# A gated attention and feed-forward kernel: the feed-forward stage written out, and two weight chunks split ahead of it

## The reference, cut to what matters

```
# x: [16, 512, 512], ctx: [16, 77, 512], float32 throughout
x = x + tanh(g_xattn) * attention(layernorm(x), ctx)       # 16 heads of 32
x = x + tanh(g_ffn) * ffn(layernorm(x))

def ffn(x):                                     # 512 -> 2048 -> 512
    hidden = x @ W1 + b1
    q = hidden + (cos(theta)*w_real + sin(theta)*w_imag) * w_imag * sin(theta + 0.1*hidden) * 0.1
    return relu(q) @ W2 + b2
```

## Time and profile before

| | |
|---|---|
| median of 3 runs | 2230.28 us (2228.26 to 2232.8) |
| the profiled execution | 2231.27 us, of which the span is 2229.5 us |
| PE, PEld busy | 98%, 82% of the span |
| DVE, ACT, POOL busy | 65%, 54%, 18% of the span |
| mean granted TensorE clock | 0.997 |
| feed-forward stage | from 812.7 us to the end |

### The profile page before, as it was taken

How to read it: one execution, slowest core, us unless ns; L and a number is a source line. 1 busy time by engine, 2 the same in 40 slices (tenths; PEclk the granted TensorE clock), 3 DMA queues, 4 the chain that set the end, 5 groups by cost and what they waited for, 6 DMA issues and landing times.

```text
span 2229.5 us, 30530 instructions
## 1 busy us (share of the span) xinstructions
PE 2183.2 (98%) x10385; PEld 1825.2 (82%) x10385; DVE 1438.1 (65%) x2596; ACT 1211.1 (54%) x3571; POOL 397.8 (18%) x329
## 2 busy tenths in 40 slices
PE   8989999999999989999999999999999999999999
PEld 6778888888888867888888788788888878888887
DVE  4566776676677648656656666566566566665654
ACT  3477777777777746444454444444444444544444
POOL 4033343333333311101101001011011010010110
PEclk9999999999999999999999999999999999999999
DMA  7513233333323334312223123122131231231210
GB/s 223 184 38 98 81 87 87 99 83 83 99 80 88 92 127 113 76 53 61 64 51 76 58 57 76 58 38 75 44 72 57 57 77 57 57 76 54 41 38 19
DMA packets 267311, 170.29 MB, mean 76 GB/s; under 512 B 189124, under 2 KB 203817, under 8 KB 267167
## 3 DMA queue, kind: packets, MB, share of 16 engines
q1 hardware_dynamic: 265775, 167.62, 28.2%
q0 software_dynamic: 960, 0.64, 0.2%
q10 hardware_dynamic: 432, 0.04, 0.0%
HBM read 108.86 MB, written 59.38 MB: 75 GB/s over the span
## 4 chain that ended last, share of the span: by engine, by line
PE 60%; DVE 1%; ACT 1%; DMA 1%; issue 0%; SPq 0%; ACTq 0%
PE m_bank L56 30%; PE pair_bank L56 30%; DVE w_split L1355 0%; DMA w_chunk<-in_L_ffn_W_dram 0%; DMA quad_scratch<-x_in 0%; DVE hidden L1388 0%; ACT relu L1315 0%; DVE turns L1384 0%; SPq L1199 0%; ACT hidden L1324 0%; ACT turns L1326 0%; DVE sine L1381 0%; DVE stats L173 0%; ACT w_split L1311 0%; DVE relu L1371 0%
## 5 line engine op out<-in xcount | busy, mean ns | idle before, releaser
L56 PE MATMUL m_bank<-xT,w_split 128*128 128x512 f32 x3072 | 740.7, 390 | 13.3 <-issue 9.4
L56 PE MATMUL pair_bank<-w_split,relu 128*128 128x512 f32 x3072 | 738.5, 389 | 3.6 <-DVE relu L1371 3.5
L56 PEld LDWEIGHTS m_bank<-xT,w_split 128*128 128x128 f32 x3072 | 577.5, 188 | 135.7 <-issue 11.5
L56 PEld LDWEIGHTS pair_bank<-w_split,relu 128*128 128x128 f32 x3072 | 576.2, 188 | 125.5 <-issue 3.8
L1331 ACT ACTIVATE sine<-turns 128x512 f32<-128x512 f32 x256 | 161.8, 632 | 386.2 <-DVE turns L1384 386.2
L1007 ACT ACTIVATE exps<-pair_bank,exp_bias 128x77 f32<-128x77 f32 x1024 | 319.5, 368 | 61.6 <-DVE exp_bias L1053 61.5
L1315 ACT ACTIVATE relu<-hidden 128x512 fp32r<-128x512 f32 x256 | 161.9, 632 | 348.3 <-PE m_bank L56 265.0
L1371 DVE SCALAR_TENSOR_TENSOR relu<-hidden,relu 128x512 fp32r<-128x512 f32 x256 | 181.2, 708 | 212.6 <-ACT relu L1315 212.6
L1388 DVE SCALAR_TENSOR_TENSOR hidden<-sine,sine_gain,hidden 128x512 f32<-128x512 f32 x256 | 197.2, 770 | 169.9 <-ACT sine L1331 169.9
L1007 ACT ACTIVATION_READ_ACCUMULATOR exps<-pair_bank,exp_bias 128x1 f32 x1024 | 255.4, 249 | 0.0
L193 POOL TENSOR_TENSOR rstd<-var_eps,minus_half 128x4 f32<-128x4 f32 x32 | 38.3, 1196 | 1202.2 <-DVE var_eps L189 1202.2
(11 more groups left out here) (117 smaller groups left out, 1918.8 us busy)
## 6 DMA issues: line engine op xcount, KB each, us to landing
x_in<-in_x_dram SPq DMA_DIRECT2D x16, 1024.0 KB, 5.7
residual<-in_x_dram SPq DMA_DIRECT2D x64, 256.0 KB, 2.7
x_scratch<-residual SPq DMA_DIRECT2D x64, 256.0 KB, 2.1
x_in<-x_scratch SPq DMA_DIRECT2D x16, 1024.0 KB, 5.6
residual<-x_scratch SPq DMA_DIRECT2D x64, 256.0 KB, 3.8
out_dram<-residual SPq DMA_DIRECT2D x64, 256.0 KB, 2.1
quad_scratch<-x_in SPq DMA_DIRECT2D x60, 256.0 KB, 5.6
x_in<-quad_scratch SPq DMA_DIRECT2D x60, 256.0 KB, 4.7
```

What stands on the lines that cost most here:

```text
L56: mm = pe.matmul(out, stationary(s), moving(m), start=first and n == 0, stop=last and n == len(PASSES) - 1)
```

## The change

1. In the feed-forward stage `over_batches` and SyncE's loop become Python loops: all 16 batches are written out for every engine.
2. Chunks 0 and 1 of w1 are split in attention. ScalarE writes their hi parts into `xT[1][0]` after its last turn; VectorE writes their lo parts into `xT[1][1]` behind the gating of output tiles 0 and 1. In the feed-forward stage ScalarE and VectorE start with chunk 2. The counts of the semaphores `chunk_hi` and `chunk_split` are raised by 3 with it.
3. TensorE takes slices 0 to 3 of batch 0 from `xT[1]`.
4. GpSimd begins the feed-forward stage with two copies, one per part, of all of `xT[1][i]` (128x2048) into `w1_split[i]`. `x_hi` of batch 1 and the first product of batch 1 wait for them (`early_kept`).

```
+        def early_parts(n):
+            return (w_chunk[n][:, :].rearrange("p (k f) -> p k f", k=KT),
+                    *(xT[1][i][:, :, HT * P * n:HT * P * (n + 1)] for i in range(2)))
...
                 over_batches(act, turn)                       # attention, ScalarE
+                for n in range(EARLY):                        # EARLY = 2
+                    raw, hi, _ = early_parts(n)
+                    act.wait_ge(chunk_loaded[n], 16)
+                    act.activation(hi, raw, ACT.Copy).then_inc(early_hi, 1)
...
                 for tile, n, bank in outputs_after():         # attention, VectorE
                     gate_output(B - 1, tile, n, bank)
+                    if tile < EARLY:
+                        raw, hi, lo = early_parts(tile)
+                        dve.wait_ge(early_hi, tile + 1)
+                        dve.tensor_tensor(lo, raw, hi.bitcast(F32), ALU.subtract).then_inc(early_split, 1)
...
-                batch(0, 0, False)                            # feed-forward, all engines
-                with eng.Fori(1, B - 2, 2) as b:
-                    batch(b, 1, False)
-                    batch(b + 1, 0, False)
-                batch(B - 1, 1, True)
+                for b in range(B):
+                    batch(b, b % 2, b == B - 1)
...
-                with sp.Fori(1, B - 2) as b:                  # SyncE
+                for b in range(1, B - 2):
...
+                pool.wait_ge(early_split, EARLY)              # GpSimd, first in its program
+                for i in range(2):
+                    pool.tensor_copy(w1_split[i][:, :, 0:EARLY * HT * P], xT[1][i][:, :, :].bitcast(F32)).then_inc(early_kept, 1)
...
-                        if f % HT == 0:                       # TensorE, first_product
+                        if f < EARLY * HT:
+                            pe.wait_ge(early_split, f // HT + 1)
+                        elif f % HT == 0:
                             pe.wait_ge(chunk_split, w1_number[f // HT] + 1)
                     elif f == 0:
                         pe.wait_ge(t_split, KT * b)
+                        if b == 1:
+                            pe.wait_ge(early_kept, 2)
...
+                        early = b == 0 and f < EARLY * HT
+                        mm = matmul3(pe, m_bank[f % 2][:, :], lambda p: (xT[1] if early else w1_split)[p][:, kt, f * P:(f + 1) * P],
...
+                    if b == 1:                                # ScalarE, x_hi
+                        act.wait_ge(early_kept, 2)
...
-                for n in range(STAGED):                       # ScalarE and VectorE, before step(0, 0)
-                    weight_lo(n)
+                for n in range(EARLY, STAGED):
+                    weight_lo(n)
+                dve.wait_ge(y_ready, NT)
```

## The result

| | before | after |
|---|---|---|
| median | 2229.27 us (4 runs) | 2215.9 us (2214.94 to 2216.13, 4 runs) |
| ratio | | 0.9942, 95% interval 0.9927 to 0.9957 |
| the profiled execution | 2231.27 us | 2215.73 us |

The kernel is 13.4 us (0.6%) faster by the medians; 2218 with a range of 2214 to 2224 was forecast. The median before has one run more here than ahead of the prediction, so it is 2229.27 and not 2230.28. In a second series, on another chip, the changed kernel had a median of 2215.09 and a ratio of 0.9931 (0.9918 to 0.9945).

What follows compares the result with a forecast made beforehand. TensorE, busy 98% of the span, was taken as the bound. 2231.27 - 11.1 (jumps) - 1.6 (start) = 2218.6, or 2217.6 for a median, stated as 2218; own range 2216 to 2221, with two rivals 2214 to 2224.

Steps and rivals of the forecast that it cites:

- The jumps: Feed-forward loop: writing it out removes TensorE's six stops at jumps, 1.86 us each, minus 11.1 us.
- control inside the body: Batch boundary inside the loop body, at 1003.59: neighbouring groups 2.72 us apart, so the jump and not the boundary costs.
- The early split is covered: End of attention: the added ScalarE copies and VectorE subtractions cost nothing; without cover 2.4 us of VectorE.
- TensorE's start: Stage opening: TensorE starts 2.37 us earlier, and its first group takes 2.97 instead of 4.63, 1.66 more.
- GpSimd's copies: Stage start: two copies of 2.79 us each lock out VectorE, leaving the first second product 1.6 us earlier, not 4.03.
- if a copy isn't near 2.8 us: Sign for GpSimd's copies at the stage's start: another length than about 2.8 us makes the prediction wrong.
- the rival in which the copies cost nothing: Stage start: copies meet no VectorE work or are fast, giving 2215.2 us; chance 12%.
- Nobody waits for these: GpSimd's queue at the stage's start: scaling of b2 and rstd can stand behind the copies without anyone waiting.
- The chain carries every shift to the 20th group: Batch 0, 825.27 to 872.94: the elementwise chain sets the pace, so moving the first second product moves everything behind equally.
- Chunk 3 isn't late: Stage start: chunk 3 lands at 823.4, before ScalarE wants it at 823.9; otherwise up to 2 us of loss.
- the clock doesn't fall in TensorE's wait: Before the first second product: TensorE idles 2.6 us, the clock may fall, and about 0.3 us would show.
- Straight code doesn't starve TensorE: Written-out stage: no stops for code; the rival has one per batch, 26 us, 2243.6 us, chance 4%.

Runs made afterwards that it cites:

- tensor_only: The kernel before with the feed-forward loop written out for TensorE alone, the other four engines keeping their loops: 2219.72 us, ratio 0.9952.
- scaling_late: The changed kernel with GpSimd's four additions of batch 0 and its scaling of b2 moved behind slice 12's mixing: 2213.78 us, ratio 0.9927.
- start_held: The changed kernel with TensorE's first product also waiting until VectorE has split chunk 2: 2219.18 us, ratio 0.995.
- copies_twice: The changed kernel with GpSimd's two copies made twice, one pair behind the other: 2216.43 us, ratio 0.9936.
- early_only: The changed kernel with the hardware loops put back, leaving the early split and GpSimd's copies: 2226.99 us, ratio 0.9987.
- copies_late: The changed kernel with GpSimd's two copies moved behind batch 0's additions and normalisation: 2216.59 us, ratio 0.9937.

## Why the prediction was right

The direction and the range came out, and three of the four parts with them. The forecast's own range, 2216 to 2221, was just missed, since one term of the sum was off. With the start at the measured 3.4 the same sum is 2231.27 - 11.1 - 3.4 - 1.0 = 2215.8, against 2215.9 measured.

- **The jumps.** Forecast 11.1, measured 11.12 between the 20th and the 509th group. The control inside the body had told rightly that it was the jump, and tensor_only showed that it was TensorE's.
- **The early split is covered.** It was, the second subtraction by only 0.1 us. In scaling_late it took 2.32 and held the next gating up by 0.2, and the last gating still came on time. ScalarE had 12.84 us of idle left behind its copies.
- **TensorE's start.** Forecast 2.37 for the wait and 1.66 for the clock. The stage opened with the barrier and the first group took 2.98; start_held shows both parts, 3.9 together.
- **GpSimd's copies: right lock, wrong size, and not the path of the sum.** This is the term that was mis-sized, and by one of the prediction's own signs ("if a copy isn't near 2.8 us") it was wrong here. I took 2.79 each, scaled from an operation with one input. The two copies and VectorE's 1.22 between them took 4.74 together, which makes 1.76 each, the rate of a memset, my lower end. The first second product came at 9.1 and not at 10.9. The start brought 3.4 us, not 1.6, and the kernel came out nearer to the rival in which the copies cost nothing (2215.2) than to the forecast. The sum had VectorE's first step begin behind both copies. With 1.76 this gives 8.9, near the 9.1 measured, but by luck: the first turns operation began at 816.10 behind ScalarE, before the second copy ended at 816.45, and 0.56 us of stretching came on top.
- **A step that failed: "Nobody waits for these", of the scaling of b2.** Nobody waits for its result, but it holds the same ports, and 0.4 us of the chain went into it.
- **The chain carries every shift to the 20th group.** It did: 3.4 us at the first second product and at the 20th group. start_held (3.9, then 3.5 to 4.2) and copies_twice (2.05, then 1.5 to 2.1) agree within the 0.7 by which two executions differ. But it isn't the elementwise chain all the way, as the prediction has it. In the kernel before, the chain that ended last goes through transfers between 849.87 and 868.36: SyncE regroups the layer-normed x, and behind that comes a chunk of the weights:

```profile
848.01 1.84 DVE x_in L198 x4
...
853.42 6.38 DMA quad_scratch<-x_in
...
861.70 6.64 DMA w_chunk<-in_L_ffn_W_dram
```

These wait for VectorE's normalisation and for each other, and so they pass a shift on.
- **Chunk 3 isn't late, the clock doesn't fall in TensorE's wait.** Both held; the wait was 0.7 us and not 2.6.
- **Straight code doesn't starve TensorE.** No stop in 15 batches.

## What to carry to other kernels

Look for gaps of the bounding engine that come back once per loop iteration without a releaser. If a boundary inside the body doesn't have them, they are the jump's, and here writing out that engine's loop alone removed them. The queue of instruction packets shows whether code is fetched there. Before a helper engine is given work that "nobody waits for", look at what VectorE does in that stretch: here two copies of 1.8 us cost 0.15 us in one place and 2.3 to 3.0 in another. When an effect is a few tenths of a percent, measure it inside the stage from the stage's first instruction, since what runs ahead of it can vary by more.

## What the hardware showed that I had not expected

- A jump of TensorE in this loop goes with three instruction packets of 16 KB. In the twelve jumps of the kernel before and of early_only it resumes 1.1 to 1.5 us behind the end of the second, and a jump costs 1.1 to 2.1 us.
- GpSimd copies 128x2048 float32 in about 1.8 us, 0.86 ns an element, as fast as it fills a tile and faster than an operation with a scalar (0.70 for 512, 1.36 ns an element).
- How long TensorE idles doesn't decide by itself whether its granted clock falls. In copies_twice it resumed behind 2.70 us at 1.00, and the group took 3.01. In copies_late it idled 1.77, after three shorter waits (1.08, 0.91 and 0.74) in the 21 us ahead, the clock fell to 0.50 and the group took 4.25. Before the change 1.4 to 1.7 us at the jumps left it at 1.00. No run here says what else counts.
